# Attention scores from three products of hi and lo parts, made on two row halves of the TensorE array

## The chip, the cores and the metric

The kernel runs on one core of a Trainium2 chip. The metric is the device time of one execution in microseconds (us), lower is better; a figure for a kernel is the median of its runs.

## What is computed

The program is a chain of six stages on an x of shape (2, 256, 256). Stages 0 and 3 are cross attentions on a context of 2 x 4096 rows, and they are what the change touches:

```python
def _L1_xattn_ref(queries, keys, values, attn_bias, Wq, Wk, Wv, Wp):   # 16 heads of 64
    q = _split_heads(queries @ Wq.T, N_HEAD, D_KEY)
    k = _split_heads(keys @ Wk.T, N_HEAD, D_KEY)
    v = _split_heads(values @ Wv.T, N_HEAD, D_VALUE)
    scores = jnp.einsum('bhqd,bhkd->bhqk', q, k) * D_MODEL ** (-0.5) + attn_bias
    weights = jax.nn.softmax(scores, axis=-1)
    out = jnp.einsum('bhqk,bhkd->bhqd', weights, v)
...
x = x + _L0_xattn_ref(_layernorm(x), ctx_1024, ...)        # 8 heads of 64, no bias
x = x + _L0_attn_ref(_layernorm(x), ...)                   # delta rule
x = x + _L0_ffn_ref(_layernorm(x), ...)                    # experts
x = x + _L1_xattn_ref(_layernorm(x), ctx_1024, ctx_1024, fside, ...)
x = x + _L1_attn_ref(_layernorm(x), ...)                   # quantised attention
x = x + _L1_ffn_ref(_layernorm(x), ...)                    # recurrent cell
```

A head's scores are 256 queries by 4096 keys over 64 dimensions.

## The kernel before

Both attentions are made by `cross_attention` (called "plain" for stage 0 and "biased" for stage 3). It goes over pairs of heads: one pass `m` is one pair of one of the two batch entries, 8 passes in the plain stage and 16 in the biased one. Each engine has its own instruction stream written by hand, and semaphores join them.

**Hi and lo parts.** Queries, keys, values and turned weights are held as two float32r parts: hi is the rounded copy, lo is the float32 sum less hi. ScalarE makes the hi parts (`keys_hi`, `values_hi`, `turned_hi`), VectorE the lo parts (`keys_lo`, `values_lo`, `turned_lo`); of the second head of a pair, chunks 1 and 3 of the keys' hi parts are ScalarE's (`BY_ACT`), chunks 0 and 2 VectorE's (L577).

**Scores.** Keys come in four chunks of 1024. `scores(m, head, i)` makes 128 queries (`qt`) by one chunk into a slot of two PSUM banks. `QS` holds a query part twice, in rows 0 to 63 and in rows 64 to 127; `KS` holds the keys' hi part in rows 0 to 63 and their lo part below. So one matmul over all 128 rows adds two products, and four matmuls of 512 columns (two query parts, two banks) give all four products of the parts. I call these four matmuls a group of scores.

**The pass on TensorE.** `attend` walks 16 steps `g` per head: turn a 128x512 piece of the exponentials three steps ahead (L394, four transposes), weigh the values with a piece (L407, four matmuls of 256 columns), and after every second step one group of scores for the next head (`beside`, L380), eight groups per `attend`. Between the two `attend`s of a pass stand the next pass's four chunks of keys (L340), and after the second its four chunks of values (L365). Slots alternate between two places, and `take` waits until the place's last content is kept: the third chunk of keys waits for `keys_kept` of the second.

```python
with pe.Fori(START, END - 1) as m:
    attend(m, 0, lambda i: scores(m, 1, i))
    keys(m + 1, 0)
    keys(m + 1, 1)
    start_attending(m, 1)
    queries(m + 1)
    project(m, 0)
    keys(m + 1, 2)
    keys(m + 1, 3)
    attend(m, 1, lambda i: scores(m + 1, 0, i))
```

The loop turns 7 times in the plain stage and 15 times in the biased one (22), with one more `attend(m, 0)` with scores behind each loop. VectorE's stream in the same order: `turned_lo` (L624) twice, then the scores out of PSUM (L609 plain, L613 biased), and so on; at the keys `keys_lo` for chunks 0 and 1, three `turned_lo`, the sums, `keys_lo` for 2 and 3, and then the next `attend`. ScalarE puts exponentials (L497) between `keys_hi` by the table `EXP_KEYS`.

**Other users of the array's parts.** The delta rule (stage 1) has matmuls over 64 rows: L941 alternates between heads in rows 0 to 63 and heads in rows 64 to 127, each with a bank of its own. Its transposes at L934 use all 128 rows. The experts' router (stage 2) goes from matmuls over 128 rows (L1425) to one over a single row (L1427) and back.

## Time and profile before

| | |
|---|---|
| runs | 2344.03 us median of 3 (2343.56 to 2344.45) |
| span of the profiled execution | 2342.4 us, 39197 instructions |
| around the span, against the median | 1.6 us |
| TensorE's matmuls busy | 2133.2 us, 91% |
| VectorE busy | 1689.1 us, 72% |
| ScalarE busy | 1246.3 us, 53% |
| GpSimd busy | 174.9 us, 7% |

The profiled execution's own time is shown as its span alone. How to read the views: times are in us from the start of the span. A row of a timeline has start, length, engine, line, operation, what it writes and reads, for TensorE the rows and columns of the array that it uses (128*128, 64*128), shapes, and how many instructions were merged into the row; in brackets the idle time before it and who ended it. PE is TensorE's matmuls, PEld its weight loads, DVE VectorE, ACT ScalarE. A matmul's end is modelled and matmuls overlap in the pipeline, so the distance between starts, and not the length, is what a matmul costs. A row of the table of stretches has its length, then the busy time and count of each engine, the granted clock of TensorE (1.00 is its higher level), and DMA. A row of the costliest groups ends in busy time and mean ns of one, then the idle time before the group.

### The profile page before, as it was taken

To read this page: it belongs to the slowest core of one execution; us is meant where nothing else is said; L and a number is where in the kernel's file an instruction comes from. 1 tells how busy PE (TensorE), PEld (TensorE's weight loads), DVE (VectorE), ACT (ScalarE), POOL (GpSimd) and SP (SyncE) were. 2 spreads that over 40 slices of the span, in tenths; PEclk is the share of its full clock that TensorE was granted. 3 is DMA by queue.
4 is the path that set the end of the run, shared out by engine and by line. 5 is a ranking of instruction groups with operands and counts; after the bars stand their busy time and mean duration, and the time that the engine had idled before them with its cause. 6 is when DMAs were issued, how large, how long until landed. Compare 5 with 4: busy or idle time off the path is not lost. (4 is left out here: it accounts for less than half of the span.)

```text
span 2342.4 us, 39197 instructions
## 1 busy us (share of the span) xinstructions
PE 2133.2 (91%) x13794; PEld 1771.3 (76%) x13794; DVE 1689.1 (72%) x2979; ACT 1246.3 (53%) x2038; POOL 174.9 (7%) x162
## 2 busy tenths in 40 slices
PE   7999999999858889899999999999999999999636
PEld 4789778977738768578877897788877887788524
DVE  5877787778586446677778777877787778777672
ACT  3665656565630135366565656565656565656401
POOL 0000000000040034000000000000000000000000
PEclk9999999999978679999999999999999999999757
DMA  2000020000010062000000000020000000000001
GB/s 92 8 12 11 4 78 11 11 4 7 5 40 1 2 222 75 5 8 12 11 4 7 11 11 4 7 83 11 8 3 11 11 11 0 11 11 5 19 0 45
DMA packets 21376, 52.35 MB, mean 22 GB/s; under 512 B 3523, under 2 KB 6100, under 8 KB 20820
## 3 DMA queue, kind: packets, MB, share of 16 engines
q1 hardware_dynamic: 20864, 51.60, 6.2%
q8 instruction: 28, 0.46, 0.1%
q10 hardware_dynamic: 468, 0.16, 0.0%
q14 instruction: 16, 0.13, 0.0%
HBM read 51.23 MB, written 0.52 MB: 22 GB/s over the span
## 5 line engine op out<-in xcount | busy, mean ns | idle before, releaser
L505 ACT ACTIVATE biased_turned_hi<-ps 128x512 fp32r<-128x512 f32 x512 | 298.9, 598 | 276.4 <-PE ps L394 273.2
L624 DVE TENSOR_TENSOR biased_turned_lo<-ps,biased_turned_hi 128x512 fp32r<-128x512 f32 x512 | 340.9, 686 | 35.0 <-ACT biased_turned_hi L505 20.0
L613 DVE CUSTOM_DVE_ANT_0 biased_scores<-ps,bias 128x1024 f32<-128x1024 f32 x256 | 312.0, 1219 | 32.3 <-issue 21.5
L497 ACT ACTIVATE biased_scores<-biased_scores,biased_ntop 128x1024 f32<-128x1024 f32 x256 | 291.9, 1146 | 75.4 <-DVE biased_ntop L619 75.4
L407 PE MATMUL ps<-biased_turned_hi,biased_values 128*128 128x256 f32 x1024 | 307.9, 324 | 15.4 <-DVE biased_turned_lo L624 15.4
L394 PE MATMUL ps<-ident,biased_scores 128*128 128x128 f32 x2048 | 299.0, 274 | 1.6 <-ACT biased_scores L497 1.6
L380 PE MATMUL ps<-biased_keys,biased_queries 128*128 128x512 f32 x1024 | 280.0, 396 | 3.1 <-DVE biased_keys L586 2.4
L394 PEld LDWEIGHTS ps<-ident,biased_scores 128*128 128x128 f32 x2048 | 244.0, 141 | 34.4 <-issue 9.8
L407 PE MATMUL ps<-biased_turned_lo,biased_values 128*128 128x256 f32 x1024 | 265.4, 282 | 0.0
L365 PEld LDWEIGHTS ps<-weights_again,context_again 128*128 128x128 f32 x2048 | 232.3, 192 | 12.0 <-DVE biased_values L592 10.3
L365 PE MATMUL ps<-weights_again,context_again 128*128 128x128 f32 x2048 | 235.6, 276 | 4.0 <-DVE biased_values L592 4.0
L340 PE MATMUL ps<-context_again,weights_again 128*128 128x512 f32 x512 | 228.1, 599 | 11.5 <-DVE biased_keys L586 9.0
L505 ACT ACTIVATE plain_turned_hi<-ps 128x512 fp32r<-128x512 f32 x256 | 149.4, 598 | 136.5 <-PE ps L394 135.0
L407 PEld LDWEIGHTS ps<-biased_turned_hi,biased_values 128*128 128x128 f32 x1024 | 194.4, 190 | 25.1 <-DVE biased_turned_lo L624 14.1
L407 PEld LDWEIGHTS ps<-biased_turned_lo,biased_values 128*128 128x128 f32 x1024 | 196.2, 192 | 4.9 <-issue 3.6
L380 PEld LDWEIGHTS ps<-biased_keys,biased_queries 128*128 128x128 f32 x1024 | 176.3, 190 | 29.2 <-DVE biased_keys L586 3.7
L592 DVE TENSOR_TENSOR biased_values<-ps,biased_values 128x1024 fp32r<-128x1024 f32 x64 | 78.4, 1224 | 161.9 <-ACT biased_values L484 161.9
L340 PEld LDWEIGHTS ps<-context_again,weights_again 128*128 128x128 f32 x512 | 95.9, 191 | 127.9 <-issue 107.5
L624 DVE TENSOR_TENSOR plain_turned_lo<-ps,plain_turned_hi 128x512 fp32r<-128x512 f32 x256 | 170.6, 686 | 24.1 <-ACT plain_turned_hi L505 16.0
L497 ACT ACTIVATE plain_scores<-plain_scores,plain_ntop 128x1024 f32<-128x1024 f32 x128 | 145.9, 1145 | 43.1 <-DVE plain_ntop L619 43.1
L609 DVE TENSOR_SCALAR_CACHE_REDUCE plain_scores<-ps 128x1024 f32<-128x1024 f32 x128 | 156.1, 1221 | 15.8 <-PE ps L380 10.9
L407 PE MATMUL ps<-plain_turned_hi,plain_values 128*128 128x256 f32 x512 | 154.1, 324 | 11.4 <-DVE plain_turned_lo L624 11.3
(362 smaller groups left out, 3271.2 us busy)
## 6 DMA issues: line engine op xcount, KB each, us to landing
context<-in_ctx_t SPq DMA_DIRECT2D x8, 1024.0 KB, 9.2
moe_w<-in_moe_w SPq DMA_DIRECT2D x32, 256.0 KB, 2.7
context_again<-in_ctx_t SPq DMA_DIRECT2D x8, 1024.0 KB, 9.8
weights_again<-in_wqkv SPq DMA_DIRECT2D x16, 384.0 KB, 3.0
bias<-in_fside SPq DMA_DIRECT2D x1, 4096.0 KB, 23.2
biased_w_out<-in_w_out SPq DMA_DIRECT2D x16, 256.0 KB, 2.6
weights<-in_wqkv SPq DMA_DIRECT2D x8, 384.0 KB, 2.9
plain_w_out<-in_w_out SPq DMA_DIRECT2D x8, 256.0 KB, 2.4
```

The costliest lines, as they stand in the source:

```text
L340: last = pe.matmul(slot("keys", j)[:, h * 512:(h + 1) * 512], W[:, 1, i, :], CT[:, i, j * KC + h * 512:j * KC + (h + 1) * 512], start=(i = ...
L365: last = pe.matmul(slot("values", j)[:, n * P:(n + 1) * P], CT[:, i, j * KC + n * P:j * KC + (n + 1) * P], W[:, 2, i, :], start=(i == 0), ...
L380: last = pe.matmul(slot(SCORES[head], i)[:, h * 512:(h + 1) * 512], QS[:, half, head, qt * P:(qt + 1) * P], KS[:, head, at:at + 512], star ...
L394: last = pe.transpose(c.ps[:, 4 + g % AHEAD, kt * S + qt * P:kt * S + (qt + 1) * P], E[:, qt, at:at + P], c.ident[:, :])
L407: last = pe.matmul(c.ps[:, 7, head * S:(head + 1) * S], VS[:, 2 * g + kt, head, :, :].rearrange("p a d -> p (a d)"), part_of[:, t % 4, kt, ...
L497: act.activation(at, at, ACT.Exp, bias=ntop[:, qt:qt + 1], accum_out=part[:, head, qt, chunk:chunk + 1]).then_inc(exp_done, 1)
L505: act.activation(PH[:, t % 4, :, :].rearrange("p a n -> p (a n)"), c.ps[:, 4 + g % AHEAD, :], ACT.Copy).then_inc(turned_high, 1)
L592: dve.tensor_tensor(VS[:, kts, :, 1, :], slot("values", j).rearrange("p (n h d) -> p n h d", h=2, d=HD), VS[:, kts, :, 0, :].bitcast(F32), ...
L609: ins = dve.tensor_scalar(at, slot(SCORES[head], i), 1.0, None, ALU.mult, ALU.max, accum_out=peak)
L613: ins = dve.tensor_tensor_reduce(at, slot(SCORES[head], i), BIAS[:, qt, chunk * KC:(chunk + 1) * KC], 1.0, -3.0e38, ALU.add, ALU.max, peak)
L624: dve.tensor_tensor(PL[:, t % 4, :, :].rearrange("p a n -> p (a n)"), c.ps[:, 4 + g % AHEAD, :], PH[:, t % 4, :, :].rearrange("p a n -> p ...
```

## The change

`scores` leaves out the product of the two lo parts and makes the three that are left (`TERMS`: hi by hi, lo by hi, hi by lo) over 64 rows each. The chunk's 1024 keys are split in halves: the first 512 lie in rows 0 to 63 of `KS`, the second 512 in rows 64 to 127, hi and lo behind each other along the free dimension. Each half has its own bank. So a group of scores has six matmuls of 64 rows and 512 columns, in three pairs (one in the upper rows, one in the lower), in place of four of 128 rows. `keys_hi` and `keys_lo` write 64x512 pieces, two where one of 64x1024 was; who makes which part and the semaphores stay. The array's tile (64 rows) differs from that of the operations before and behind a group (128 rows).

```diff
--- before.py
+++ after.py
@@ -205,7 +205,7 @@
         WO = sb("w_out", [P, 2, D])
         QS = sb("queries", [P, 2, 2, S], F32R)
         QP = sb("pair_queries", [P, 2, S], F32R)
-        KS = sb("keys", [P, 2, S2], F32R)
+        KS = sb("keys", [P, 2, 2, S2 // 2], F32R)
         VS = sb("values", [P, KT, 2, 2, HD], F32R)
         E = sb("scores", [P, 2, S2])
         PH = sb("turned_hi", [P, 4, 2, S], F32R)
@@ -250,6 +250,14 @@
             return c.ps[:, u:u + 2, :].rearrange("p a n -> p (a n)")
 
         SCORES = ("scores A", "scores B")
+        TERMS = ((0, 0), (1, 0), (0, 1))
+
+        def keys_of(head, half, part, j):
+
+            return KS[half * HD:(half + 1) * HD, head, part, j * 512:(j + 1) * 512]
+
+        def keys_sums(head, half, j):
+            return slot("keys", j)[head * HD:(head + 1) * HD, half * 512:(half + 1) * 512]
 
         def row(m):
 
@@ -374,12 +382,13 @@
                         pe.wait_ge(keys_kept, NKC * m + chunk + 1)
                         if i == 0:
                             pe.wait_ge(q_kept, 4 * m + 4)
-                    for h in range(2):
-                        at = chunk * KC + h * 512
+                    for n, (q_part, k_part) in enumerate(TERMS):
                         for half in range(2):
-                            last = pe.matmul(slot(SCORES[head], i)[:, h * 512:(h + 1) * 512],
-                                             QS[:, half, head, qt * P:(qt + 1) * P], KS[:, head, at:at + 512],
-                                             start=(half == 0), stop=(half == 1))
+                            rows = slice(half * HD, (half + 1) * HD)
+                            last = pe.matmul(slot(SCORES[head], i)[:, half * 512:(half + 1) * 512],
+                                             QS[rows, q_part, head, qt * P:(qt + 1) * P],
+                                             KS[rows, head, k_part, chunk * 512:(chunk + 1) * 512],
+                                             start=(n == 0), stop=(n == len(TERMS) - 1))
                     last.then_inc(scores_done, 1)
 
                 def turn(m, head, g):
@@ -473,11 +482,9 @@
             def _(act):
                 def keys_hi(m, j):
                     act.wait_ge(keys_done, NKC * m + j + 1)
-                    act.activation(KS[0:HD, 0, j * KC:(j + 1) * KC], slot("keys", j)[0:HD, :],
-                                   ACT.Copy).then_inc(keys_high, 1)
-                    if j in BY_ACT:
-                        act.activation(KS[0:HD, 1, j * KC:(j + 1) * KC], slot("keys", j)[HD:P, :],
-                                       ACT.Copy).then_inc(keys_high, 1)
+                    for head in range(2 if j in BY_ACT else 1):
+                        act.activation(keys_of(head, 0, 0, j), keys_sums(head, 0, j), ACT.Copy)
+                        act.activation(keys_of(head, 1, 0, j), keys_sums(head, 1, j), ACT.Copy).then_inc(keys_high, 1)
 
                 def values_hi(m, j):
                     act.wait_ge(values_done, NKC * m + j + 1)
@@ -570,21 +577,25 @@
             def _(dve):
                 def keys_lo(m, j):
 
-                    at = slice(j * KC, (j + 1) * KC)
-                    src = slot("keys", j)
+                    def low(head, half):
+                        return dve.tensor_tensor(keys_of(head, half, 1, j), keys_sums(head, half, j),
+                                                 keys_of(head, half, 0, j).bitcast(F32), ALU.subtract)
+
                     if j not in BY_ACT:
                         dve.wait_ge(keys_done, NKC * m + j + 1)
-                        dve.tensor_copy(KS[0:HD, 1, at], src[HD:P, :]).then_inc(keys_high_b, 1)
+                        dve.tensor_copy(keys_of(1, 0, 0, j), keys_sums(1, 0, j))
+                        dve.tensor_copy(keys_of(1, 1, 0, j), keys_sums(1, 1, j)).then_inc(keys_high_b, 1)
 
                     act_parts = (NKC + len(BY_ACT)) * m + j + sum(n < j for n in BY_ACT)
                     dve.wait_ge(keys_high, act_parts + 1)
-                    dve.tensor_tensor(KS[HD:P, 0, at], src[0:HD, :], KS[0:HD, 0, at].bitcast(F32), ALU.subtract)
+                    low(0, 0)
+                    low(0, 1)
                     if j in BY_ACT:
                         dve.wait_ge(keys_high, act_parts + 2)
                     else:
                         dve.wait_ge(keys_high_b, (NKC - len(BY_ACT)) * m + j + 1 - sum(n < j for n in BY_ACT))
-                    dve.tensor_tensor(KS[HD:P, 1, at], src[HD:P, :], KS[0:HD, 1, at].bitcast(F32),
-                                      ALU.subtract).then_inc(keys_kept, 1)
+                    low(1, 0)
+                    low(1, 1).then_inc(keys_kept, 1)
 
                 def values_lo(m, j):
                     kts = slice(j * (KC // P), (j + 1) * (KC // P))
```

TensorE's stream in the plain stage's loop, second step of `attend(m, 0)`, before and then after: the weighing (L407, now L416), the first group of scores beside it (L380, now L388) and the transposes behind it (L394, now L403).

```order
L407 MATMUL ps<-plain_turned_hi,plain_values 128x256
L407 MATMUL ps<-plain_turned_lo,plain_values 128x256
L322 REGISTER_ALU
L380 MATMUL ps<-plain_keys,plain_queries 128x512 x4
L394 MATMUL ps<-ident,plain_scores 128x128 x4
```

```order
L416 MATMUL ps<-plain_turned_hi,plain_values 128x256
L416 MATMUL ps<-plain_turned_lo,plain_values 128x256
L330 REGISTER_ALU
L388 MATMUL ps<-plain_keys,plain_queries 128x512 x6
L403 MATMUL ps<-ident,plain_scores 128x128 x4
```

The group stands at the same place between the same neighbours; it has six matmuls where it had four.

VectorE's stream in the biased stage's loop, `keys_lo(m + 1, 0)`, before and then after: the second head's hi part (CAST), and the lo parts of both heads.

```order
L577 CAST biased_keys<-ps 64x1024 [waits cross_keys_done]
L580 ISA
L581 TENSOR_TENSOR biased_keys<-ps,biased_keys 64x1024 [waits cross_keys_high]
L585 ISA
L586 TENSOR_TENSOR biased_keys<-ps,biased_keys 64x1024 [waits cross_keys_high_b]
```

```order
L586 CAST biased_keys<-ps 64x512 [waits cross_keys_done]
L587 CAST biased_keys<-ps 64x512
L590 ISA
L581 TENSOR_TENSOR biased_keys<-ps,biased_keys 64x512 [waits cross_keys_high]
L581 TENSOR_TENSOR biased_keys<-ps,biased_keys 64x512
L596 ISA
L581 TENSOR_TENSOR biased_keys<-ps,biased_keys 64x512 [waits cross_keys_high_b]
L581 TENSOR_TENSOR biased_keys<-ps,biased_keys 64x512
```

Each operation on 1024 columns is now two on 512, with the wait on the first of the two; the order of the parts is the same.

## Rows read from the trace of the kernel before

**Rows 1.** The page's first part: busy time and share of each engine
```profile
PE 2133.2 (91%) x13794; PEld 1771.3 (76%) x13794; DVE 1689.1 (72%) x2979; ACT 1246.3 (53%) x2038; POOL 174.9 (7%) x162
```

**Rows 2.** One biased pass in four stretches: attend, values, attend, keys
```profile
1500.83:1522.86 22.03, 21.37 (x151) 19.23 (x150) 19.97 (x37) 10.64 (x18) 0.86 (x1) 1.00 0.00 0
1522.86:1539.70 16.84, 16.64 (x145) 16.19 (x144) 7.88 (x14) 12.43 (x20) 0.00 (x0) 1.00 0.04 16
1539.70:1560.53 20.83, 20.83 (x151) 19.10 (x150) 17.86 (x35) 10.21 (x17) 0.00 (x0) 1.00 0.56 220
1560.53:1577.77 17.24, 16.64 (x54) 8.62 (x53) 13.57 (x20) 14.41 (x23) 3.28 (x4) 1.00 0.00 0
```

**Rows 3.** Timeline of TensorE's matmuls, one two-step unit of an attend
```profile
1506.18 0.28 PE L407 MATMUL ps<-biased_turned_lo,biased_values 128*128 128x256 f32 x1
1506.30 1.09 PE L380 MATMUL ps<-biased_keys,biased_queries 128*128 128x512 f32 x4
1507.22 0.60 PE L394 MATMUL ps<-ident,biased_scores 128*128 128x128 f32 x4
...
1509.05 1.09 PE L380 MATMUL ps<-biased_keys,biased_queries 128*128 128x512 f32 x4
```

**Rows 4.** Timeline of TensorE's weight loads, the same group of scores
```profile
1506.18 0.77 PEld L380 LDWEIGHTS ps<-biased_keys,biased_queries 128*128 128x128 f32 x4
```

**Rows 5.** Timeline of VectorE, two scores out of PSUM behind a backlog
```profile
1505.59 1.22 DVE L613 CUSTOM_DVE_ANT_0 biased_scores<-ps,bias 128x1024 f32<-128x1024 f32 x1
...
1507.94 1.22 DVE L613 CUSTOM_DVE_ANT_0 biased_scores<-ps,bias 128x1024 f32<-128x1024 f32 x1
```

**Rows 6.** Timeline of the matmuls where the delta rule changes to 64 rows
```profile
712.88 0.27 PE L934 MATMUL ps<-ident,delta_fractal 128*128 128x128 f32 x1
713.08 1.16 PE L941 MATMUL ps<-delta_channels_first 64*128 64x128 f32 x16
```

**Rows 7.** The same place, loads and matmuls, in a shorter stretch
```profile
713.08 0.41 PEld L941 LDWEIGHTS ps<-delta_channels_first 64*128 64x128 f32 x6 [0.17 <-issue]
713.08 0.49 PE L941 MATMUL ps<-delta_channels_first 64*128 64x128 f32 x4
```

**Rows 8.** Timeline of the matmuls, values: 64 of 128 columns over 128 rows
```profile
1522.86 7.31 PE L365 MATMUL ps<-weights_again,context_again 128*128 128x128 f32 x64
```

**Rows 9.** Timeline of the router, matmuls over one row
```profile
836.55 0.60 PE L1427 MATMUL ps<-moe_router_b,ones 1*128 1x15 f32 x2
```

**Rows 10.** Timeline of the router, weight loads for 128 rows behind them
```profile
837.09 0.93 PEld L1425 LDWEIGHTS ps<-moe_router_w,XNT 128*128 128x128 f32 x4
```

**Rows 11.** The page's costliest groups: pieces of 512 columns, and weight loads
```profile
L505 ACT ACTIVATE biased_turned_hi<-ps 128x512 fp32r<-128x512 f32 x512 | 298.9, 598 | 276.4 <-PE ps L394 273.2
L624 DVE TENSOR_TENSOR biased_turned_lo<-ps,biased_turned_hi 128x512 fp32r<-128x512 f32 x512 | 340.9, 686 | 35.0 <-ACT biased_turned_hi L505 20.0
...
L394 PEld LDWEIGHTS ps<-ident,biased_scores 128*128 128x128 f32 x2048 | 244.0, 141 | 34.4 <-issue 9.8
...
L380 PEld LDWEIGHTS ps<-biased_keys,biased_queries 128*128 128x128 f32 x1024 | 176.3, 190 | 29.2 <-DVE biased_keys L586 3.7
```

**Rows 12.** Timeline of TensorE, the two waits of a pass in the biased stage
```profile
1571.20 7.13 PE L340 MATMUL ps<-context_again,weights_again 128*128 128x512 f32 x16 [0.60 <-DVE biased_keys L586]
...
1582.66 0.38 PE L407 MATMUL ps<-biased_turned_hi,biased_values 128*128 128x256 f32 x1 [0.66 <-DVE biased_turned_lo L624]
```

**Rows 13.** The list of waits, TensorE at the third chunk of keys
```profile
PE ps L340 <- DVE biased_keys L586: 9.0, 15, 0.6
```

**Rows 14.** Timeline of ScalarE at the keys
```profile
1567.64 1.00 ACT L476 ACTIVATE biased_keys<-ps 64x1024 fp32r<-64x1024 f32 x1
...
1569.72 1.57 ACT L505 ACTIVATE biased_turned_hi<-ps 128x512 fp32r<-128x512 f32 x3
```

**Rows 15.** Timeline of VectorE at the keys
```profile
1569.91 1.23 DVE L586 TENSOR_TENSOR biased_keys<-ps,biased_keys 64x1024 fp32r<-64x1024 f32 x1
1571.17 1.89 DVE L624 TENSOR_TENSOR biased_turned_lo<-ps,biased_turned_hi 128x512 fp32r<-128x512 f32 x3
```

## The prediction

> **What bounds the kernel now.** I read the page's first part, then one pass in four stretches, then the timeline of one unit of `attend` engine by engine. The page gives TensorE 91% [rows 1]. The stretches of one biased pass add up to 76.94 us (22.03 + 16.84 + 20.83 + 17.24); TensorE is busy for 75.49 of them at the granted clock 1.00, its higher level of 2.4 GHz, and VectorE for 59.28 [rows 2]. 24 such passes (8 plain ones taken as equal) are 1847 us, most of the span. So the question is what the change does to TensorE's stream, and whether another engine is close behind.
>
> A unit of two steps with one group of scores takes 2.75 us on TensorE: the group starts at 1506.30 and the next at 1509.05. The group itself takes 0.92 us (1506.30 to 1507.22, when the transposes start), so 0.23 us for each matmul of 512 columns [rows 3]. Its weight loads cost nothing: they start at 1506.18, together with the last matmul of the weighing, while the array works [rows 3, 4]. VectorE, when it works off a backlog, needs 2.35 us for the same unit (1505.59 to 1507.94) [rows 5]. So TensorE sets the pace in `attend`, with 0.40 us of room down to VectorE, and anything added to a group of scores there is added to the time.
>
> **The change part by part.** *Pairs.* The trace has a model for them: L941 alternates between upper and lower 64 rows with a bank each. 16 matmuls of 128 columns, eight pairs, lie in 1.16 us [rows 6], and the first two pairs in 0.49 [rows 7]. With 0.27 for the length of the last (as for the single matmul ahead of them), the second pair starts 0.22 behind the first, and the other six pitches take 1.16 - 0.27 - 0.22 = 0.67, so 0.11 each; the first has 0.10 to 0.11 more. The values' matmuls, 128 columns over all rows, take (7.31 - 0.28) / 63 = 0.11 each [rows 8]. So a pair costs as much as one full matmul: the halves run together. Three pairs of 512 columns then cost 3 x 0.23 = 0.69 us against 0.92.
>
> *Entering.* When the array's tile changes from 128 rows to 64, the next weights are not loaded under the last matmul. The last transpose of L934 ends at 713.15 (712.88 + 0.27) and the loads of L941 start at 713.08, after 0.17 us in which the loader idles with no releaser, and the first pair takes some 0.10 us more than the later ones, which I read as the wait for its weights [rows 6, 7]. So the load starts 0.07 before the modelled end of the last matmul. In `attend` the last matmul ahead of a group starts at 1506.18 and lasts 0.28; the load would start at 1506.39 and the group at 1506.49, against 1506.30 now [rows 3]: **+0.19 us**.
>
> *Leaving.* The way back to 128 rows costs the same: the router's one-row matmuls end at 837.15 and the loads for 128 rows start at 837.09 [rows 9, 10]. A last matmul of 512 columns starts 0.23 before its successor does now and its length is 1.09 - 3 x 0.23 = 0.40 [rows 3], so the load comes 0.33 behind its start. Transposes load faster (141 ns against 190) [rows 11], so for them I put 0.05 in place of 0.10: 0.38 against 0.23, **+0.15**. Six of eight groups have transposes behind them. The other two, ahead of weighing and ahead of keys or values, have the full load, +0.20. The mean is +0.16.
>
> *A group* costs 0.19 + 0.69 + 0.16 - 0.92 = **+0.12 us** on TensorE: what the third pair saves is less than two changes of tile. Groups in a running `attend`: 8 x (15 + 31) = 368 (the loops' two per pass, 22 passes, and one behind each loop). The 16 groups ahead of the loops follow each other without a change of tile, while VectorE takes 1.2 us for each [rows 5], so I cost them at nothing; without that cover they would save 16 x 0.23 = 3.7. 368 x 0.12 = **+44.2 us**.
>
> *What waits absorb.* In each of 22 passes TensorE waits twice in front of VectorE. At the third chunk of keys it idles 0.60 us, in 15 of 15 biased passes [rows 12, 13]; the leaving cost of the group ahead (0.20) falls into it, since the chain that ends the wait hangs on that group's end and not on TensorE's next start: -4.4. At the third step of `attend(m, 1)` it idles 0.66 for `turned_lo` [rows 12], into which that stretch's first group falls: -2.6.
>
> *Keys.* Pieces of 64x512 replace those of 64x1024. ScalarE's hi part took 1.00; three pieces of 512 lie in 1.57, 0.52 each [rows 14], alone 0.60 [rows 11]: two take 1.05 to 1.20, so +0.05 to +0.20. VectorE's took 1.23; three pieces of 512 lie in 1.89, 0.63 each [rows 15], alone 0.69 [rows 11]: two take 1.26 to 1.37, +0.03 to +0.14. I take +0.10 for both, between the ends, since the second piece has no wait of its own but lies in other partitions. Both waits above end on these chains. Chunk 1 is kept at 1571.14 (1569.91 + 1.23) and the matmuls start at 1571.20 [rows 12, 15]; behind the exponentials' start ScalarE has two hi parts on that path (one in front of the exponentials, the first head's of chunk 1, 1567.64) and VectorE two lo parts: +0.4. The `turned_lo` of the other wait stands in VectorE's queue behind chunk 3's lo parts, released by one hi part: +0.3. TensorE waits for each, and the transposes, weighing and the next scores wait behind it. 22 x 0.7 = **+15.4** (ends: 22 x 0.2 = 4 and 22 x 1.1 = 25). The same chain at the two stages' starts: +1.
>
> *Sum* against the profiled span: 2342.4 + 44.2 - 4.4 - 2.6 + 15.4 + 1 = 2396.0; with the 1.6 us that lie between this span and the median, 2397.6. I say **2398 us**, 2.3% slower. A change of 0.2% (4.7 us) is about what a measurement of this kernel can tell from none.
>
> **A rule weighed.** At L941 each pair's loads start with the previous pair's matmuls, in the same rows, and the pitch stays 0.11 [rows 6, 7]. The Trainium skill (TensorE: Matmul & The Clock Gate, Part 3, The mechanism) says that a weight load overlaps matmuls in flight only where it targets other row groups. By that rule the second and third pair would each expose a load; the trace disagrees. The rival for it is below.
>
> **The rivals.** *The change of tile is free here* (faster). Then a group costs 0.69, -0.23 x 368 = -85. Back come the first groups' gain in front of `turned_lo` (22 x 0.23 = 5), some 3 at the other `attend`, where that part is ready only just in time, and the keys' 15: 2344 - 85 + 23 = 2282. VectorE's 2.35 would still be under 2.52. It decides once the two changes together cost under about 0.19 us per group (0.23 less the keys' 15 us over 368 groups). Both changes of tile in the rows, one each way, start their loads 0.06 to 0.07 before the end of the last matmul, so I give it 0.07.
> *Only the loads are exposed, not the drain*: entry 0.10, exit 0.06, a group 0.85, -26 in all; with the keys' +16 and the absorbed parts (about +2) some 2336, up to 2346 at the keys' dear end. Chance 0.04, half of it within 0.2%. For it: both places in the rows have transposes or one-row matmuls around the change, not matmuls of 256 and 512 columns.
> *Each pair exposes its loads*: two more times 0.10 per group, 368 x 0.20 = +74: 2472. Float32r at 64 rows isn't in the trace, float32 is. Chance 0.03. The skill's rule above would end here.
> *The halves don't run together*: six matmuls of 0.23 and the two changes are 1.73, +0.81 per group, +298, with less absorbed about 2655. Against it stands L941. For it: 512 columns of float32r over half the array are not in the trace. Chance 0.04.
> *The change doesn't reach the array*: the stream shows six matmuls where four were, so no.
>
> **How the numbers follow.** My forecast has 0.82. Its terms move: a pair 0.22 to 0.24 (368 x 0.03 = 11 each way), changes 0.03 each way (11), keys 4 to 25. That is 2365 to 2430, and I widen it to 2352 to 2445 for terms that add up or that I missed. The other cases lie outside, 0.18 in all. Faster by over 0.2%: 0.07 + 0.02 = 0.09. Within: 0.02. Slower: 0.82 + 0.03 + 0.04 = 0.89.
>
> **What the new profile would show.** Starts of the six matmuls in pairs some 7 to 10 ns apart, pairs 0.23 apart; in front of each group and behind it weight loads that idle 0.15 to 0.3 us with no releaser; a group from its weighing's end to the transposes' start about 1.04 in place of 0.92; a unit of 2.87 in place of 2.75; VectorE idle in each unit; the wait at the third chunk of keys about 0.8. The prediction is wrong if loads for 64 rows start under the 128-row matmuls, if pairs are apart by 0.3 or more, or if the wait at the keys grows by over 1 us.

## The result

The changed kernel takes **2413.89 us** (median of 4 runs, 2413.38 to 2414.99), the kernel before 2344.24 beside it (median of 4 runs): a ratio of 1.0296, with a 95% interval of 1.0283 to 1.0310. That is 69.7 us or 3.0% slower. The forecast was 2398 us, 54 us slower, with a range of 2352 to 2445.

The page's first part after the change, which answers to [rows 1]:

```profile
span 2412.0 us, 41117 instructions
...
PE 2175.8 (90%) x14562; PEld 1693.5 (70%) x14562; DVE 1740.7 (72%) x3219; ACT 1271.0 (53%) x2182; POOL 174.9 (7%) x162
```

TensorE is busy for 42.6 us more, with 768 more matmuls; VectorE for 51.6 us and ScalarE for 24.7 us more. The span grew by 69.6 us (2342.4 to 2412.0). So more than TensorE's own work was added.

One biased pass in four stretches, in the order attend, keys, attend, values (columns: the stretch and its length, the length again with the work of matmuls, then weight loads, VectorE, ScalarE and GpSimd in it, the granted clock, the DMA share and GB/s):

```profile
1503.80:1525.51 21.71, 21.71 (x168) 17.36 (x166) 18.17 (x35) 10.21 (x17) 0.00 (x0) 1.00 0.06 18
1525.51:1543.47 17.96, 16.74 (x55) 8.72 (x53) 14.32 (x27) 14.96 (x27) 3.28 (x4) 1.00 0.00 0
1543.47:1566.87 23.40, 22.31 (x166) 17.48 (x164) 21.01 (x40) 11.07 (x20) 0.86 (x1) 1.00 0.00 0
1566.87:1583.71 16.84, 16.64 (x145) 16.18 (x144) 7.87 (x14) 12.46 (x20) 0.00 (x0) 1.00 0.06 16
```

The values' stretch is as long as before (16.84). The `attend` ahead of the keys went from 20.83 to 21.71, the keys from 17.24 to 17.96, the other `attend` from 22.03 to 23.40 [rows 2]. The pass went from 76.94 to 79.91: +2.97 us, which makes 65 us of the 69.6 over 22 passes. The granted clock is 1.00 in all four stretches, its level of 2.4 GHz, as before, so the clock has no part in it.

**The group of scores.** TensorE's matmuls in one unit of two steps (start, length, engine, line, operation, weights' rows and columns, moving tile, count; the idle time before, where there is one, in brackets):

```profile
1505.35 0.96 PE L388 MATMUL ps<-biased_keys,biased_queries 64*128 64x512 f32 x6
...
1508.02 0.28 PE L416 MATMUL ps<-biased_turned_lo,biased_values 128*128 128x256 f32 x1
1508.22 0.98 PE L388 MATMUL ps<-biased_keys,biased_queries 64*128 64x512 f32 x6
1509.13 0.66 PE L403 MATMUL ps<-ident,biased_scores 128*128 128x128 f32 x4
```

The unit takes 1508.22 - 1505.35 = 2.87 us, against 2.75 in [rows 3]. From the last matmul of the weighing (1508.02) to the transposes (1509.13) it is 1.11 us, against 1.04 (1506.18 to 1507.22): +0.07 at this place, and the rest of the 0.12 lies behind the transposes' start. The weight loads of the same place:

```profile
1508.22 0.53 PEld L388 LDWEIGHTS ps<-biased_keys,biased_queries 64*128 64x128 f32 x6
1509.13 0.31 PEld L403 LDWEIGHTS ps<-ident,biased_scores 128*128 128x128 f32 x3 [0.37 <-issue]
```

The loads for 64 rows start at 1508.22. The last matmul of 128 rows ends at 1508.02 + 0.28 = 1508.30 by its modelled end, so the load starts 0.08 us before that end, where before it started together with that matmul [rows 4]. On the way back the loader idles for 0.37 us, released by nothing that the profile shows. Cut off after two and after four matmuls, the group shows its pairs:

```profile
1508.22 0.50 PE L388 MATMUL ps<-biased_keys,biased_queries 64*128 64x512 f32 x2
```

```profile
1508.22 0.74 PE L388 MATMUL ps<-biased_keys,biased_queries 64*128 64x512 f32 x4
```

Two matmuls lie in 0.50 us, four in 0.74, six in 0.98: each further pair adds 0.24 us, as much as one full matmul of 512 columns. The first pair is dearer. A matmul of 512 columns that waits for no weights is 0.40 us long (1.09 - 3 x 0.23, [rows 3]), so the second pair starts 0.74 - 0.40 = 0.34 behind the first and the third 0.24 behind the second. With that the cost of the two changes of tile splits as follows. On the way in the group starts 0.20 us behind the last matmul of the weighing (1508.02 to 1508.22), where it was 0.12, and its first pair takes 0.10 more: +0.18. On the way back the transposes start 1509.13 - 1508.22 - 0.34 - 0.24 = 0.33 behind the third pair, 0.09 more than a pair takes, and from their start to the weighing it is 0.41 in place of 0.35: +0.15.

**The waits.** TensorE from the keys to the third step of the next `attend`:

```profile
1525.51 7.13 PE L348 MATMUL ps<-context_again,weights_again 128*128 128x512 f32 x16
...
1536.90 7.13 PE L348 MATMUL ps<-context_again,weights_again 128*128 128x512 f32 x16 [1.22 <-DVE biased_keys L581]
...
1548.92 0.38 PE L416 MATMUL ps<-biased_turned_hi,biased_values 128*128 128x256 f32 x1 [1.09 <-DVE biased_turned_lo L635]
```

At the third chunk of keys TensorE now idles 1.22 us where it was 0.60, and at the third step, for `turned_lo`, 1.09 where it was 0.66 [rows 12]. The list of waits (us in total, times, longest) says that it is so in each pass:

```profile
PE ps L416 <- DVE biased_turned_lo L635: 21.9, 17, 5.3
PE ps L348 <- DVE biased_keys L581: 18.3, 15, 1.2
```

The first of the two also counts single waits elsewhere; the second was 9.0 us in 15 passes [rows 13]. VectorE at the keys:

```profile
1529.24 0.69 DVE L586 CAST biased_keys<-ps 64x512 fp32r<-64x512 f32 x1 [1.89 <-PE ps L348]
1529.95 0.69 DVE L587 CAST biased_keys<-ps 64x512 fp32r<-64x512 f32 x1
...
1534.05 2.79 DVE L581 TENSOR_TENSOR biased_keys<-ps,biased_keys 64x512 fp32r<-64x512 f32 x4 [0.57 <-ACT biased_keys L487]
```

Four pieces of 64x512 lie in 2.79 us, so 0.70 each: they follow each other without any overlap, and so do the two CASTs (1529.24 and 1529.95, 0.71 apart). Two operations of 1024 columns took 1.23 each [rows 15], so VectorE's part of this chain went from 2.46 to 2.79.

ScalarE's hi part of the first chunk, with the exponential behind it, in the kernel before and then in the changed one:

```profile
1564.48 1.00 ACT L476 ACTIVATE biased_keys<-ps 64x1024 fp32r<-64x1024 f32 x1
1565.38 1.13 ACT L497 ACTIVATE biased_scores<-biased_scores,biased_ntop 128x1024 f32<-128x1024 f32 x1
```

```profile
1529.95 0.59 ACT L487 ACTIVATE biased_keys<-ps 64x512 fp32r<-64x512 f32 x1
1530.56 1.15 ACT L504 ACTIVATE biased_scores<-biased_scores,biased_ntop 128x1024 f32<-128x1024 f32 x1
```

Before, the exponential starts 0.90 us behind the start of the hi part, 0.10 before that ends. Now it starts 0.61 behind a piece of 0.59, and the first of the two pieces starts at 1529.37: 1.19 us in place of 0.90. So the pieces cost 0.18 us there, and the overlap with the exponential behind them, which is gone, another 0.10.

### The profile page after: what moved, and what is told of

It is laid out like the page before. It is cut to its first block and busy times, and to the rows that moved or that the text cites. A ratio compares the mean times of both kernels' runs of the same rounds, so it can differ in the third digit from the quotient of the medians.

```text
span 2412.0 us, 41117 instructions
## 1 busy us (share of the span) xinstructions
PE 2175.8 (90%) x14562; PEld 1693.5 (70%) x14562; DVE 1740.7 (72%) x3219; ACT 1271.0 (53%) x2182; POOL 174.9 (7%) x162
## 5 line engine op out<-in xcount | busy, mean ns | idle before, releaser
L504 ACT ACTIVATE biased_scores<-biased_scores,biased_ntop 128x1024 f32<-128x1024 f32 x256 | 292.2, 1147 | 74.1 <-DVE biased_ntop L630 73.3
L416 PE MATMUL ps<-biased_turned_hi,biased_values 128*128 128x256 f32 x1024 | 311.3, 327 | 21.9 <-DVE biased_turned_lo L635 21.9
L403 PE MATMUL ps<-ident,biased_scores 128*128 128x128 f32 x2048 | 309.4, 279 | 1.6 <-ACT biased_scores L504 1.6
L403 PEld LDWEIGHTS ps<-ident,biased_scores 128*128 128x128 f32 x2048 | 229.1, 141 | 78.2 <-issue 67.1
L416 PE MATMUL ps<-biased_turned_lo,biased_values 128*128 128x256 f32 x1024 | 264.6, 281 | 0.0
L388 PE MATMUL ps<-biased_keys,biased_queries 64*128 64x512 f32 x1536 | 249.0, 430 | 4.0 <-DVE biased_keys L581 3.2
L373 PEld LDWEIGHTS ps<-weights_again,context_again 128*128 128x128 f32 x2048 | 231.1, 192 | 16.4 <-DVE biased_values L603 10.3
L416 PEld LDWEIGHTS ps<-biased_turned_hi,biased_values 128*128 128x128 f32 x1024 | 194.6, 190 | 41.3 <-issue 20.8
L416 PEld LDWEIGHTS ps<-biased_turned_lo,biased_values 128*128 128x128 f32 x1024 | 196.2, 192 | 3.6 <-issue 3.6
L581 DVE TENSOR_TENSOR biased_keys<-ps,biased_keys 64x512 fp32r<-64x512 f32 x256 | 176.3, 689 | 20.2 <-ACT biased_keys L487 16.6
L416 PE MATMUL ps<-plain_turned_hi,plain_values 128*128 128x256 f32 x512 | 155.8, 327 | 13.0 <-DVE plain_turned_lo L635 13.0
```

The costliest lines, as they stand in the source:

```text
L373: last = pe.matmul(slot("values", j)[:, n * P:(n + 1) * P], CT[:, i, j * KC + n * P:j * KC + (n + 1) * P], W[:, 2, i, :], start=(i == 0), ...
L388: last = pe.matmul(slot(SCORES[head], i)[:, half * 512:(half + 1) * 512], QS[rows, q_part, head, qt * P:(qt + 1) * P], KS[rows, head, k_pa ...
L403: last = pe.transpose(c.ps[:, 4 + g % AHEAD, kt * S + qt * P:kt * S + (qt + 1) * P], E[:, qt, at:at + P], c.ident[:, :])
L416: last = pe.matmul(c.ps[:, 7, head * S:(head + 1) * S], VS[:, 2 * g + kt, head, :, :].rearrange("p a d -> p (a d)"), part_of[:, t % 4, kt, ...
L504: act.activation(at, at, ACT.Exp, bias=ntop[:, qt:qt + 1], accum_out=part[:, head, qt, chunk:chunk + 1]).then_inc(exp_done, 1)
L581: return dve.tensor_tensor(keys_of(head, half, 1, j), keys_sums(head, half, j), keys_of(head, half, 0, j).bitcast(F32), ALU.subtract)
```

## The experiments

Two theories stood at first. **One**: the keys' pieces cost twice what I had put, and the scores' tile changes cost what I had put. **Two**: the keys are as forecast, and something at the scores (a group's edges, or what waits absorb) is missing. The runs take the change apart. Each ratio is to runs of the kernel before on the same chip.

### The keys' pieces alone, written where they were before

`scores` is unchanged and `KS` keeps its layout; only the pieces are halved.

```diff
-                    dve.tensor_tensor(KS[HD:P, 0, at], src[0:HD, :], KS[0:HD, 0, at].bitcast(F32), ALU.subtract)
+                    for half in range(2):
+                        at = slice(j * KC + half * 512, j * KC + (half + 1) * 512)
+                        dve.tensor_tensor(KS[HD:P, 0, at], src[0:HD, half * 512:(half + 1) * 512],
+                                          KS[0:HD, 0, at].bitcast(F32), ALU.subtract)
```

> The kernel before, with each of the keys' 64x1024 operations on ScalarE and VectorE made as two of 64x512 to the same places; the scores as before. Theory K (the pieces of the keys were under-priced in the forecast, 0.7 us a pass, and cost about 1.4): pieces follow each other without overlap, 0.70 us each on VectorE and 0.59 on ScalarE, the wait at the third chunk of keys grows from 0.60 to about 1.4 us and that for turned_lo from 0.66 to about 1.1; 22 x 1.4 = +30 us, about 2375. Rival T (the pieces cost what was forecast, and the 16 us over the forecast come from the scores on TensorE): +15 us, about 2359.

Measured: 2353.35 us, ratio 1.0039 (1.0027 to 1.0052), span +9.0 us. Both theories had more (the hi parts and the CAST are halved in the same way as the lo part above). VectorE at the keys:

```profile
1492.54 1.30 DVE L580 CAST biased_keys<-ps 64x512 fp32r<-64x512 f32 x2 [1.70 <-PE ps L340]
...
1497.16 1.28 DVE L587 TENSOR_TENSOR biased_keys<-ps,biased_keys 64x512 fp32r<-64x512 f32 x2 [0.63 <-ACT biased_keys L478]
```

Here two pieces lie in 1.28 to 1.30 us, where the changed kernel's take 0.70 each. ScalarE's first pair, and then four pieces:

```profile
1492.85 1.05 ACT L478 ACTIVATE biased_keys<-ps 64x512 fp32r<-64x512 f32 x2
...
1496.06 2.17 ACT L478 ACTIVATE biased_keys<-ps 64x512 fp32r<-64x512 f32 x4
```

Four lie in 2.17 us; two operations of 1024 columns lie in 2.05 in the trace of the kernel before (1.00 for one [rows 14], and a little between them), four of the changed kernel's pieces 4 x 0.59 = 2.36. The first pair is the plainest on ScalarE: two pieces in 1.05 us with 0.57 for one alone, so the second comes 0.48 behind the first. In this run both pieces of a pair read and write the same partitions. So halving an operation is cheap, +0.05 to +0.07 us, and what makes it dear in the changed kernel must be where the pieces lie. The span rose by 9.0 us all the same: the wait at the third chunk of keys is 0.84 us here and the one for `turned_lo` 0.85, in place of 0.60 and 0.66.

### The new scores alone

The pairs of 64 rows, with keys made as before. The lower rows multiply the lo parts of the keys, so the scores are not those of the reference; the stream of instructions is the changed kernel's.

```diff
-                    for h in range(2):
-                        at = chunk * KC + h * 512
+                    for n, q_part in enumerate((0, 1, 0)):
                         for half in range(2):
-                            last = pe.matmul(slot(SCORES[head], i)[:, h * 512:(h + 1) * 512],
-                                             QS[:, half, head, qt * P:(qt + 1) * P], KS[:, head, at:at + 512],
-                                             start=(half == 0), stop=(half == 1))
+                            rows = slice(half * HD, (half + 1) * HD)
+                            at = chunk * KC + half * 512
+                            last = pe.matmul(slot(SCORES[head], i)[:, half * 512:(half + 1) * 512],
+                                             QS[rows, q_part, head, qt * P:(qt + 1) * P], KS[rows, head, at:at + 512],
+                                             start=(n == 0), stop=(n == 2))
```

> The kernel before with its keys untouched (hi parts in rows 0 to 63, lo parts below, 64x1024 operations), but the scores made as six matmuls of 64 rows in three pairs. What is changed in the computation: the lower rows then multiply lo parts of the keys where the changed kernel has hi parts, so these scores are other numbers; the work and its order are those of the changed kernel. Theory K: a group costs 0.12 us more, 368 groups 44 us, less about 7 us that the two waits absorb: +37 us, about 2381; together with e1 it gives the +70 of the change. Rival T: +53 us, about 2397. If neither side holds, the two do not add up to 70.

Measured: 2387.29 us, ratio 1.0183 (1.0166 to 1.0200), span 2385.3, +42.9 us. My terms give 44.2 for the groups. Less the 2.6 that I let the `turned_lo` wait absorb that is 41.6, less the 4.4 at the keys as well 37.2. The wait for `turned_lo` fell from 0.66 to 0.54 as put. The one at the keys did not shrink by 0.20:

```profile
1506.99 7.13 PE L340 MATMUL ps<-context_again,weights_again 128*128 128x512 f32 x16
...
1517.73 2.84 PE L340 MATMUL ps<-context_again,weights_again 128*128 128x512 f32 x6 [0.57 <-DVE biased_keys L587]
```

It is 0.57 after 0.60. What starts the chain stands in ScalarE's stream:

```profile
1512.88 1.14 ACT L498 ACTIVATE biased_scores<-biased_scores,biased_ntop 128x1024 f32<-128x1024 f32 x1
...
1514.16 1.02 ACT L477 ACTIVATE biased_keys<-ps 64x1024 fp32r<-64x1024 f32 x1
```

The hi part of chunk 1 starts at 1514.16. The exponential ahead of it has ended by then (1512.88 + 1.14 = 1514.02), and TensorE's chunk is done at 1506.99 + 7.13 = 1514.12. So in this run the chain that ends the wait hangs on TensorE's own keys, which the group's leaving cost pushes back. In the kernel before it was a close thing:

```profile
1560.53 7.03 PE L340 MATMUL ps<-context_again,weights_again 128*128 128x512 f32 x16
...
1566.51 1.13 ACT L497 ACTIVATE biased_scores<-biased_scores,biased_ntop 128x1024 f32<-128x1024 f32 x1
```

There the exponential ahead ends at 1567.64, and the hi part begins at 1567.64 [rows 14]: ScalarE went from one to the other without a pause, and its stream of exponentials hangs on the group of scores, as I had read it. But TensorE's second chunk was done at 1567.56, just 0.08 earlier, and in this run a hi part that waits for TensorE starts 0.04 behind its end. So there were some 0.04 us of room, and a delay of 0.20 on TensorE could fall into the wait for that much only. With the scores alone the absorbed -4.4 shrinks to 22 x 0.03 = -0.7.

### Three full matmuls, and four products in pairs

The first leaves out the product of the queries' lo part for the second 512 keys of each chunk: three matmuls over all 128 rows, and no change of tile. The second adds the product of the two lo parts to the changed kernel.

```diff
-                        for half in range(2):
+                        for half in range(2 - h):
...
-                                             start=(half == 0), stop=(half == 1))
+                                             start=(half == 0), stop=(half == 1 - h))
```

```diff
-        TERMS = ((0, 0), (1, 0), (0, 1))
+        TERMS = ((0, 0), (1, 0), (0, 1), (1, 1))
```

> The kernel before with three matmuls of 128 rows in a group in place of four; left out is the product with the queries' lo part for the second half of each chunk. It is the saving of a matmul's time without a change of tile. My theory: a group falls from 0.92 to 0.69 us, 368 x 0.23 = -85, and some 8 us come back at the two places where TensorE then waits earlier for VectorE: about 2267. Rival: VectorE is a close second bound (a unit at over 2.6 us in the long run, not 2.35), then the gain stays under 50 us, over 2295.

> The changed kernel with the product of the two lo parts put back, four pairs in a group: what a pair costs. My theory: a pair takes 0.235 us as a full matmul does, the changes of tile stay two a group: 368 x 0.235 less 5 us in front of turned_lo = +81 on the changed kernel, about 2495, and the two changes of tile show as the difference to a group of four full matmuls. Rival (a part of the cost sits in the first pair or grows with the number of pairs, because their weights are late): a pair costs 0.3 us or more, over 2515.

Measured: three full matmuls 2280.72 us, ratio 0.9725 (0.9709 to 0.9741), span 2279.7. Four products in pairs 2496.19 us, ratio 1.0645 (1.0628 to 1.0663), span 2493.9. TensorE's matmuls, three full ones:

```profile
1540.57 0.39 PE L407 MATMUL ps<-biased_turned_hi,biased_values 128*128 128x256 f32 x1 [0.90 <-DVE biased_turned_lo L624]
...
1546.34 0.86 PE L380 MATMUL ps<-biased_keys,biased_queries 128*128 128x512 f32 x3
...
1548.87 0.86 PE L380 MATMUL ps<-biased_keys,biased_queries 128*128 128x512 f32 x3
```

and four products in pairs:

```profile
1554.61 1.19 PE L388 MATMUL ps<-biased_keys,biased_queries 64*128 64x512 f32 x8
...
1557.69 1.20 PE L388 MATMUL ps<-biased_keys,biased_queries 64*128 64x512 f32 x8
```

The units are 1548.87 - 1546.34 = 2.53 and 1557.69 - 1554.61 = 3.08 us (most of this run's are 3.10 to 3.12). The changed kernel's has 2.87. So a group of three pairs is 0.34 us dearer than three full matmuls in a row: this is what entering and leaving the 64-row tile costs, against 0.35 forecast (0.19 + 0.16). The spans say nearly the same, with the waits in it: the run with the new scores alone less this one is 2385.3 - 2279.7 = 105.6 us over 368 groups, 0.29 each. A pair more costs (2493.9 - 2412.0) / 368 = 0.22 us in the spans, and 0.24 if the wait for `turned_lo`, which fell from 1.09 to 0.86 in each pass, is added back. The three-matmul kernel missed its forecast by 14 us: of the 85 us, 22 came back, where I had put 8. The wait for `turned_lo` is longer (0.90 in the rows, from 0.66), and so are the first two units of each `attend`, measured against those of the kernel before less one matmul: 3.68 and 2.67 us in the `attend` with this wait in place of 3.45 and 2.52, and 2.80 and 2.66 in the other in place of 2.59 and 2.52. With the longer wait included that is 0.73 us in a pass, 16 of the 22. I read it as `attend` getting there before VectorE does. The other 6 I haven't located. Its 63 us is what the third product saved would be worth here if it cost no tile change. It is no version of this kernel, as it leaves out part of a product.

### The new keys alone, written as the changed kernel writes them

The changed kernel with four matmuls over all 128 rows in a group. The rows hold other products than the reference's; the stream outside `scores` is the changed kernel's.

```diff
-                    for n, (q_part, k_part) in enumerate(TERMS):
-                        for half in range(2):
-                            rows = slice(half * HD, (half + 1) * HD)
-                            last = pe.matmul(slot(SCORES[head], i)[:, half * 512:(half + 1) * 512],
-                                             QS[rows, q_part, head, qt * P:(qt + 1) * P],
-                                             KS[rows, head, k_part, chunk * 512:(chunk + 1) * 512],
+                    for h in range(2):
+                        for part in range(2):
+                            last = pe.matmul(slot(SCORES[head], i)[:, h * 512:(h + 1) * 512],
+                                             QS[:, part, head, qt * P:(qt + 1) * P],
+                                             KS[:, head, h, chunk * 512:(chunk + 1) * 512],
...
```

> The changed kernel's keys (64x512 pieces that go to the upper and the lower rows in turn) with four matmuls of 128 rows and 512 columns in a group, as before, and no change of tile. What is changed in the computation: these matmuls add products of the two halves of a chunk, so the scores are other numbers; the work is that of the kernel before in the scores and of the changed one in the keys. e1 showed that pieces which stay in the same partitions overlap (pitch 0.61 us on VectorE, 0.48 on ScalarE), and in the changed kernel they don't (0.70 and 0.59). Theory P (the alternation between partitions costs it): e1's +9 and 22 x 0.7 = 15 more, about 2369, and with e2's +43 that gives the +70. Rival (the remainder comes only when slower keys and slower scores meet): as e1, about 2353.

Measured: 2374.57 us, ratio 1.0144 (1.0125 to 1.0163), span 2372.8, +30.4 us. The same number of pieces of the same size cost 9.0 us when the two of a pair stay in their partitions, and 30.4 us when they alternate between rows 0 to 63 and 64 to 127. The waits say where:

```profile
1514.16 7.13 PE L348 MATMUL ps<-context_again,weights_again 128*128 128x512 f32 x16 [1.39 <-DVE biased_keys L580]
...
1526.18 0.39 PE L415 MATMUL ps<-biased_turned_hi,biased_values 128*128 128x256 f32 x1 [1.21 <-DVE biased_turned_lo L634]
```

At the third chunk of keys it is 1.39 us, from 0.60, and for `turned_lo` 1.21, from 0.66. The two make 1.34 of the 30.4 / 22 = 1.38 us per pass, where my prediction had 0.7.

The two halves of the change, alone, make 30.4 + 42.9 = 73.3 us; together they make 69.6. Most of the missing 3.7 us lie at the third chunk of keys, where the changed kernel waits 1.22 and this run 1.39. ScalarE's stream in the changed kernel shows why:

```profile
1531.71 1.13 ACT L504 ACTIVATE biased_scores<-biased_scores,biased_ntop 128x1024 f32<-128x1024 f32 x1
...
1532.84 0.57 ACT L486 ACTIVATE biased_keys<-ps 64x512 fp32r<-64x512 f32 x1
```

The hi part of chunk 1 starts where the exponential ahead of it ends, 1532.84, and TensorE's second chunk was done by 1525.51 + 7.13 = 1532.64. The slower hi part of chunk 0 has pushed ScalarE's stream back, by 0.29, so the chain now hangs on that stream with 0.2 us of room left (0.4 in this run), and the group's leaving cost on TensorE falls into the wait: 22 x 0.17 = 3.7 us, against 0.7 with the scores alone. That is 3.0 of the 3.7. So the absorbed part at the keys is there in the changed kernel and all but absent in the scores alone. Of the two theories the first had the size of the keys right, though not the reason, and the scores alone (42.9 us) came out between the two, since next to nothing of the absorbed part at the keys is there without the slower keys.

### Whole chunks in one row half

If the partitions are the cost, then a layout that needs no pieces should give the 30 us back: even chunks lie in the upper rows, odd ones in the lower, so `keys_hi` and `keys_lo` make 64x1024 again. A group takes 512 keys of each of two chunks; the values' tiles and the bias are read in the matching order, and TensorE waits for both chunks of a pair.

```diff
-            return KS[half * HD:(half + 1) * HD, head, part, j * 512:(j + 1) * 512]
+            return KS[j % 2 * HD:(j % 2 + 1) * HD, head, part, j // 2 * KC:(j // 2 + 1) * KC]
...
-                    low(0, 0)
-                    low(0, 1)
+                    low(0)
...
+        def value_tile(n):
+            block, within = divmod(n, 8)
+            return (block // 2 * 2 + within // 4) * 8 + block % 2 * 4 + within % 4
```

> The changed kernel with the same three products on row halves, but the upper rows hold the even chunks of keys and the lower rows the odd ones, so the keys' operations are 64x1024 again, as before; a group of scores then has 512 keys of each of two chunks, and bias and values are taken in that order. Theory P: the keys' cost goes, what is left is the cost of the scores alone as in e2, about 2387. Rival: the bias read in two stretches costs VectorE time in each group, then over 2395.

Measured: 2389.22 us, ratio 1.0197 (1.0178 to 1.0215), span 2388.8. The wait at the third chunk of keys is back at 8.4 us in 15 passes, 0.6 at most, as before the change. The time is 46.4 us above the kernel before beside it (2342.87), where the run with the new scores alone was 43.1 above its own (2344.19), and the intervals of the two ratios overlap. So this layout makes the products of the reference at about the price of the scores alone: it gives back 2412.0 - 2388.8 = 23 us of the changed kernel's time, nearly all of what the keys cost on top of the scores (69.6 - 42.9 = 27), and the scores' tile changes stay.

### Fewer tile changes

Per group 0.34 us go to the tile. Two groups behind each other share an entry and an exit, so the next three kernels put both groups of a four-step stretch side by side: in the changed kernel, in the one with whole chunks, and, as a control with no tile change to save, in the kernel before.

```diff
-                        if g % 2 and beside:
-                            beside(g // 2)
+                        if g % 4 == 3 and beside:
+                            beside(g // 2 - 1)
+                            beside(g // 2)
...
-                        if g % 2 and beside:
-                            beside(g // 2 - 1)
+                        if g >= 5 and g % 4 == 1 and beside:
+                            beside(g // 2 - 2)
+                            beside(g // 2 - 1)
...
+                        beside(NSC - 2)
```

> The changed kernel with two groups of scores behind every fourth step of attend in place of one behind every second, so half as many changes of tile; VectorE takes two scores in a row. My theory (0.35 us for the two changes of tile around a group): 184 times 0.35 less, -64 us, 2350, and up to 10 more where VectorE's two scores in a row keep turned_lo waiting: 2350 to 2360. Rival (the cost sits in the pairs themselves, 0.04 us in each, and not at the changes): as the changed kernel, 2414 or more.

> e6 and e7 together. If their savings add: 2414 - 27 - 60 = about 2327, under both kernels. Rival (with TensorE faster, the two scores in a row on VectorE become the bound of an attend): over 2344.

> The kernel before with two groups of scores behind every fourth step, as e7 has it on the changed kernel; no change of tile here. e7 came out at 2509, not 2355. Theory W (the regrouping itself costs waits for VectorE, at the ends of each attend and in front of turned_lo, and these hide what fewer changes of tile save): this kernel too is far slower than before, by 100 us or more, and the difference between e7 and this one is far below the 70 us of the change. Rival (the regrouping costs nothing by itself and a longer run of pairs is what is dear): about 2345, and e7 is 160 above it.

Measured: in the changed kernel 2508.95 us, ratio 1.0712 (1.0693 to 1.0731); with whole chunks 2466.52, ratio 1.0535 (1.0511 to 1.0558); in the kernel before 2469.98, ratio 1.0534 (1.0516 to 1.0551). All are slower than with one group every second step. TensorE's matmuls, two groups each fourth step in the changed kernel:

```profile
1559.26 0.39 PE L416 MATMUL ps<-biased_turned_hi,biased_values 128*128 128x256 f32 x1 [0.72 <-DVE biased_turned_lo L636]
...
1559.93 1.65 PE L388 MATMUL ps<-biased_keys,biased_queries 64*128 64x512 f32 x12
...
1563.38 0.60 PE L403 MATMUL ps<-ident,biased_scores 128*128 128x128 f32 x4
1563.98 0.39 PE L416 MATMUL ps<-biased_turned_hi,biased_values 128*128 128x256 f32 x1
...
1565.56 1.65 PE L388 MATMUL ps<-biased_keys,biased_queries 64*128 64x512 f32 x12
...
1579.06 1.12 PE L348 MATMUL ps<-context_again,weights_again 128*128 128x512 f32 x2 [0.89 <-DVE biased_top L625]
```

The four-step stretch from 1559.93 takes 5.63 us, against 2 x 2.87 = 5.74. It holds a wait that the view doesn't mark, since the modelled end of the transposes covers it: the weighing at 1563.98 starts 0.60 behind the transposes (1563.38), where without a wait it is 0.35. Without these 0.25 us the stretch is 5.38, so the shared change of tile does save about its 0.34, and 0.11 of it are left. The edges pay more: 0.72 and, at the end of the `attend`, 0.89 for scores that VectorE has not taken out of PSUM yet. The waits of this run and then, in a fence of its own, of the kernel before with two groups:

```profile
PE ps L416 <- DVE biased_turned_lo L636: 62.6, 64, 5.2
...
PE ps L348 <- DVE biased_top L625: 13.4, 15, 0.9
```

```profile
PE ps L407 <- DVE biased_turned_lo L625: 51.8, 64, 5.6
```

Where `turned_lo` was waited for 17 times, it is 64 times now, four in each of 16 passes, and as often in the kernel before with two groups, where the regrouping alone costs 2468.5 - 2342.4 = 126 us. In the changed kernel it costs 2502.1 - 2412.0 = 90, and with whole chunks 2459.2 - 2388.8 = 70. The last is the one to set beside the kernel before, as the keys are made in the same way in both: the 56 us between 126 and 70 are what sharing a tile change gave, of 4 x 46 x 0.34 = 63 us that it could. In the changed kernel it gave 36; where the other 20 went I haven't located. Either is far from what the uneven work for VectorE takes: two scores in a row on VectorE are 2.4 us during which no `turned_lo` comes.

A last arrangement spreads the groups 1, 2, 2, 2, 1 over an `attend`, and takes each out of PSUM between two `turned_lo`.

```diff
-                        if g % 2 and beside:
-                            beside(g // 2)
+                        for i in {1: (0,), 5: (1, 2), 9: (3, 4), 13: (5, 6), 15: (7,)}.get(g, ()):
+                            if beside:
+                                beside(i)
...
-                        if g % 2 and beside:
-                            beside(g // 2 - 1)
+                        for i in {3: (0,), 7: (1,), 8: (2,), 11: (3,), 12: (4,), 15: (5,)}.get(g, ()):
+                            if beside:
+                                beside(i)
...
+                        beside(NSC - 2)
```

> e6 (whole chunks on row halves) with the groups of an attend as 1, 2, 2, 2, 1, behind steps 1, 5, 9, 13 and 15, and VectorE's scores kept apart by a turned_lo: five runs of pairs in place of eight, so three times two changes of tile fewer in each of 46 attends. My theory (0.35 us for each two): 46 x 3 x 0.35 = -48 us from e6's 2389, 2341, and up to 15 more of waits: 2341 to 2356. Rival (waits take all of it, as in e7): 2389 or more.

Measured: 2441.02 us, ratio 1.0411 (1.0394 to 1.0428): better than the other regroupings, worse than whole chunks with one group per two steps (2389.22). TensorE's matmuls:

```profile
1523.20 1.67 PE L400 MATMUL ps<-biased_keys,biased_queries 64*128 64x512 f32 x12
...
1527.60 0.60 PE L415 MATMUL ps<-ident,biased_scores 128*128 128x128 f32 x4
1528.63 0.39 PE L428 MATMUL ps<-biased_turned_hi,biased_values 128*128 128x256 f32 x1 [0.43 <-DVE biased_turned_lo L644]
...
1529.30 1.65 PE L400 MATMUL ps<-biased_keys,biased_queries 64*128 64x512 f32 x12
```

Four steps take 6.10 us; without waits it should be 5.74 - 0.34 = 5.40. The rows put 0.43 down to the wait for `turned_lo`, counted from the modelled end of the transposes. By the starts it is more: the weighing comes 1.03 behind the transposes (1527.60 to 1528.63), where it is 0.36 without a wait, so 0.67 are lost, and 5.43 are left.

## Why the prediction was right, and where its sizes were off

The direction was right and the measured time is in the range, 16 us above the forecast of 2398.

- **Pairs: right.** Put at 0.23 us per pair (that the halves run together was read from the delta rule's 128 columns), measured 0.24 within a group and 0.22 to 0.24 by the run with four products. The halves run together at 512 columns too, so the rival with halves one behind the other is out.
- **Tile changes: right.** Put at 0.19 + 0.16 = 0.35 us per group, measured 0.34 (2.87 against 2.53), and by the starts some 0.18 in front and 0.15 behind. The load for 64 rows starts 0.08 us before the modelled end of the last matmul, as at the delta rule [rows 6, 7]. The unit came out at 2.87 as put. The rival with free changes is out: it would be the three-full-matmul run, 2280.72, with the keys' cost on top. So is the one in which only the loads are exposed, whose unit would be 2.68. So is the rule that each pair exposes its loads: the pairs lie 0.24 apart, and the loads of a group take 0.53 us inside its 0.98.
- **Absorbed in front of `turned_lo`, -2.6: right.** With the scores alone the wait fell by 0.12.
- **Absorbed at the keys, -4.4: nearly right in the changed kernel, with a margin that I had not looked at.** The wait is 0.17 shorter than with the new keys alone (1.22 against 1.39), so 3.7 us. With the scores alone it is 0.03, because TensorE's own second chunk is done just 0.08 us before ScalarE's stream is ready for it. I had read the chain that ends the wait and not asked which one ends next. That the change slows the keys too, and so makes the room for this term, is luck: the prediction didn't have it.
- **Keys, +15.4: mis-sized by half.** The two waits and the chains to them were right, and 0.7 us per pass became 30.4 / 22 = 1.38: +0.79 at the third chunk of keys, where I had 0.4, and +0.55 for `turned_lo`, where I had 0.3. I took +0.10 for a pair of pieces on each engine, halfway between pieces that overlap and pieces that don't; they don't overlap at all: 0.70 each on VectorE, +0.17 for a pair, and 0.59 each on ScalarE, +0.18. I had named the reason for doubt (other partitions) and then split the difference. And on ScalarE the exponential behind the pieces lost its overlap of 0.10, which my sum doesn't have. With the +1 at the stages' starts the forecast had 16.4 of the 30.4 us, so this is 14.0. It was also more than the upper end of 25. The wait at the third chunk was to be about 0.8 us in the new profile and is 1.22.
- *The balance, in spans.* 2412.0 less 2396.0 is 16.0. The keys make 14.0 of it. The scores on top of them made 69.6 - 30.4 = 39.2, forecast 44.2 - 4.4 - 2.6 = 37.2: the other 2.0. The range held because the scores' terms used little of their room; the keys' term alone was past its own end.

So in each of 368 groups the change saves 0.23 us of matmul and pays 0.34 for the tile: +0.11 to 0.12, some 43 us of the 69.6. The rest, some 27, comes from the layout that the pairs ask of the keys, and whole chunks in a row half give back 23 of it. Nothing that I ran makes the same products faster than the kernel before: with whole chunks a group of pairs would need its tile changes to cost under 0.23 us, or to be shared by more products without making the work for VectorE uneven, and the regroupings fail at the latter.

## What to carry to other kernels

Row halves pay only if the matmuls saved are longer than entering and leaving the tile: here 0.34 us, or one and a half matmuls of 512 columns, per switch there and back. Before splitting an operation of VectorE or ScalarE, look whether the pieces keep their partitions: then a split costs little (9 us here, against 30). To find what a waiting engine's chain hangs on, add start and duration of each candidate and see which ends last before the chain's first operation starts. Then look at the one that ends next: a cost that a wait should absorb goes into it only as far as that one leaves room, here 0.04 us with the old keys and 0.4 with the new ones.

## What the runs showed of the hardware that I had not expected

- In these runs pieces of 64x512 overlap with the one behind them only where both keep their partitions. On VectorE the second of a pair then comes 0.61 us behind the first (1.30 less 0.69), on ScalarE 0.48 (1.05 less 0.57). In the changed kernel the two pieces of a pair read the same rows of PSUM and write other rows of `KS`: 0.70 and 0.59 apart. A change of the output rows is enough for that. Where the input rows change and the output rows stay (the first run's two heads on ScalarE), four pieces in 2.17 us leave 2.17 - 2 x 0.48 - 0.59 = 0.62 for the step between the heads, so that seems to be enough too. The number of partitions need not be the same: before the change an exponential over all 128 rows starts 0.90 us behind a hi part of 1.00 us in rows 0 to 63, and after it 0.61 behind a piece of 0.59 us written to rows 64 to 127. Both fit an overlap that asks for the same first partition; no run here tests that by itself.
- Matmuls of 64 rows and 512 columns in float32r, one in each row half with its own bank, take together what one over 128 rows takes: 0.24 us against 0.23. The first pair behind 128-row matmuls takes 0.34.
- Moving two groups together in the kernel before cost 126 us, 5.3%, with the same work on each engine: VectorE is busy for 72% of the span, and yet the kernel stands or falls with when its work comes.
